# Attention layer 1 of a graph network on one Trainium2 core: the query and key product with its operands exchanged

## The reference

```python
def rgat_conv(x, W, q, k, b, src, dst, etype, heads, out_ch, n_nodes):
    xr = jnp.einsum('nd,rdf->rnf', x, W)          # 3 relations x 256 nodes x 768
    oi = xr[etype, dst]
    oj = xr[etype, src]
    qi = oi @ q                                    # 4 query numbers per row of xr
    kj = oj @ k                                    # 4 key numbers per row of xr
    alpha = jax.nn.leaky_relu(qi + kj, NEG_SLOPE)
    m = jax.ops.segment_max(alpha, dst, num_segments=n_nodes)
    e = jnp.exp(alpha - m[dst])
    z = jax.ops.segment_sum(e, dst, num_segments=n_nodes)
    a = e / (z[dst] + EPS)
    msg = (a[:, :, None] * oj.reshape(-1, heads, out_ch)).reshape(-1, heads * out_ch)
    out = jax.ops.segment_sum(msg, dst, num_segments=n_nodes)
    return out + b
...
h = rgat_conv(x, W1, q1, k1, b1, src, dst, edge_type, HEADS1, OUT1, n)
h = jax.nn.elu(h)
out = rgat_conv(h, W2, q2, k2, b2, src, dst, edge_type, HEADS2, OUT2, n)
```

## Time and profile before

| | |
|---|---|
| median of 3 runs | 1147.63 us (1140.77 to 1148.91) |
| the profiled execution's own time | 1147.76 us |
| its span in the profile | 1146.0 us |
| PE busy | 1086.9 us (95%) |
| VectorE busy | 766.9 us (67%) |
| ScalarE busy | 572.0 us (50%) |
| mean granted TensorE clock | 0.981 of full speed |

### The profile page before, as it was taken

How to read it: one execution, slowest core, us unless ns; L and a number is a source line. 1 busy time by engine, 2 the same in 40 slices (tenths; PEclk the granted TensorE clock), 3 DMA queues, 4 the chain that set the end, 5 groups by cost and what they waited for, 6 DMA issues and landing times.

```text
span 1146.0 us, 17627 instructions
## 1 busy us (share of the span) xinstructions
PE 1086.9 (95%) x7440; PEld 902.1 (79%) x7440; DVE 766.9 (67%) x1082; ACT 572.0 (50%) x602; POOL 180.1 (16%) x96
## 2 busy tenths in 40 slices
PE   7999998999899999998999989899999999999987
PEld 5889986444699964446679889858999999999984
DVE  7994763888643148885355374755888888888752
ACT  0433225888433258884234353424666666666640
POOL 2434602555100015552000000000000000000000
PEclk9999999999899999999999799999999999999998
DMA  8043285211044372210234103507777777777720
GB/s 292 11 132 119 84 270 154 60 56 56 1 166 166 120 220 57 74 56 1 83 132 179 49 1 131 196 1 259 255 234 250 244 249 246 247 246 240 246 98 28
DMA packets 82322, 163.47 MB, mean 143 GB/s; under 512 B 4034, under 2 KB 60126, under 8 KB 81950
## 3 DMA queue, kind: packets, MB, share of 16 engines
q1 hardware_dynamic: 80736, 151.86, 39.8%
q0 software_dynamic: 1504, 10.44, 3.5%
HBM read 158.64 MB, written 0.80 MB: 139 GB/s over the span
## 4 chain that ended last, share of the span: by engine, by line
PE 66%; DVE 20%; ACT 7%; issue 4%; DMA 1%; POOL 1%; SPq 0%; DVEq 0%; ACTq 0%; POOLq 0%
PE PS L977 12%; PE PS L835 7%; PE PS L717 6%; PE PS L469 6%; PE PS L631 4%; PE PS L733 4%; PE PS L456 4%; DVE Wlo L1783 3%; PE PS L607 3%; PE PS L991 3%; PE PS L960 3%; ACT Whi L1308 3%; PE PS L538 2%; DVE PRD L1554 2%; PE PS L896 2%
## 5 line engine op out<-in xcount | busy, mean ns | idle before, releaser
L1783 DVE TENSOR_TENSOR Wlo<-W,Whi 128x2304 fp32r<-128x2304 f32 x68 | 173.8, 2557 | 43.4 <-ACT Whi L1308 43.4
L1308 ACT CAST Whi<-W 128x2304 fp32r<-128x2304 f32 x68 | 144.4, 2125 | 0.1
L977 PE MATMUL PS<-Whi,Mhi 128*128 128x384 f32 x408 | 139.6, 342 | 3.5 <-DVE Mlo L1812 3.5
L977 PE MATMUL PS<-Wlo,Mhi 128*128 128x384 f32 x408 | 136.6, 335 | 0.0
L977 PE MATMUL PS<-Whi,Mlo 128*128 128x384 f32 x408 | 136.6, 335 | 0.0
L428 POOL TENSOR_TENSOR PRDP<-arena 128x1024 f32<-128x1024 f32 x48 | 114.6, 2388 | 122.8 <-PE PS L733 88.3
L717 PE MATMUL PS<-QH,SEL 128*128 128x512 f32 x384 | 116.8, 426 | 9.6 <-DVE arena L1554 3.6
L717 PEld LDWEIGHTS PS<-QH,SEL 128*128 128x128 f32 x384 | 65.4, 190 | 60.6 <-DVE PRD L1554 22.7
L1169 ACT ACTIVATE arena<-PS 128x1024 f32<-128x1024 f32 x96 | 98.5, 1026 | 27.7 <-PE PS L717 27.7
L1169 ACT ACTIVATE PS<-PS 128x1024 f32<-128x1024 f32 x96 | 98.0, 1020 | 0.0
L977 PEld LDWEIGHTS PS<-Whi,Mhi 128*128 128x128 f32 x408 | 76.7, 188 | 8.3 <-DVE Mlo L1812 8.3
(11 more groups left out here) (274 smaller groups left out, 2403.2 us busy)
## 6 DMA issues: line engine op xcount, KB each, us to landing
W<-in_L_rel SPq DMA_DIRECT2D x68, 1152.0 KB, 5.6
W<-in_W_rel SPq DMA_DIRECT2D x6, 2304.0 KB, 9.2
W<-in_W SPq DMA_DIRECT2D x6, 2304.0 KB, 8.5
arena<-in_qU SPq DMA_DIRECT2D x96, 128.0 KB, 2.6
W<-in_WqT SPq DMA_DIRECT2D x4, 2304.0 KB, 9.2
W<-in_W_root SPq DMA_DIRECT2D x2, 2304.0 KB, 13.4
W<-in_WgT SPq DMA_DIRECT2D x2, 2304.0 KB, 9.0
QH<-QH POOLq DMA_DIRECT2D x2, 1536.0 KB, 10.0
```

What stands on the lines that cost most here:

```text
L977: mm = pe.matmul(PS[:, 4 + s % 2, 0:HALF], MS[a][mb][:, k, j * P:(j + 1) * P], WS[b][w % 3][:, k, :], start=n == 0, stop=n == 17)
L1308: nc.scalar.copy(WS[0][w % 3][:], W[(FIRST34 + r) % 2][:, :, q * HALF:(q + 1) * HALF]).then_inc(w_hi, 1)
L1783: V.tensor_tensor(WS[1][w % 3][:], W[(FIRST34 + r) % 2][:, :, q * HALF:(q + 1) * HALF], WS[0][w % 3][:].bitcast(F32), ALU.subtract).then_i ...
```

## The change

`queries_keys(r)` makes the 128 x 8 block of `qk1` stationary and lets a 128 x 256 block of `XT` move, so that its result is eight rows of 256 nodes (partitions 0 to 7 of bank 3 for relations 0 and 1, of bank 4 for relation 2). VectorE negates these rows into a new tile `qkR` in two pieces. `spread_keys` of layer 1 selects one row of `qkR` with a broadcast column of the identity (8 x 128, stationary) while 8 x 256 blocks of `qkR` move. The queries are turned back by six transposes (`turn_queries`), issued between the spreads of head 0 and head 1, and VectorE copies them to `qkN`. `turn_rows(2)` is issued ahead of `queries_keys(1)` instead of behind it. Layer 2 keeps its code.

```diff
+        qkR = put("qkR", [2 * HEADS1, R3 * NODES], F32, 36)
...
-            pool.wait_ge(qk_done, 1)
+            pool.wait_ge(qk_done, R3)
...
-                for t in range(NT):
-                    at = (t * R3 + r) * 2 * HEADS1
-                    for k in range(KC):
-                        mm = pe.matmul(PS[:, 3, at:at + 2 * HEADS1], XT[:, r, k, t * P:(t + 1) * P], qk1[:, k, :],
-                                       start=k == 0, stop=k == KC - 1)
-                return mm
+                for k in range(KC):
+                    mm = pe.matmul(PS[0:2 * HEADS1, 3 + r // 2, (r % 2) * NODES:(r % 2 + 1) * NODES], qk1[:, k, :], XT[:, r, k, :],
+                                   start=k == 0, stop=k == KC - 1)
+                mm.then_inc(qk_done, 1)
+
+            def turn_queries():
+
+                for c in range(R3 * NT):
+                    r, t = divmod(c, NT)
+                    mm = pe.transpose(PS[:, 6, 2 * HEADS1 * (R3 * t + r):2 * HEADS1 * (R3 * t + r + 1)],
+                                      qkR[:, c * P:(c + 1) * P], ident[0:2 * HEADS1, 0:2 * HEADS1])
+                mm.then_inc(rows_turned, 1)
...
                     queries_keys(0)
+                    turn_rows(2)
                     queries_keys(1)
-                    turn_rows(2)
-                    queries_keys(2).then_inc(qk_done, 1)
+                    queries_keys(2)
...
-                    pe.wait_ge(qkn_copied, 1)
+                    pe.wait_ge(qkr_copied, 2)
...
-                    for c in range(R3 * NT):
+                    for r in range(R3 if l == 0 else 0):
+                        mm = pe.matmul(PS[:, 4 - h % 2 * 2 + r // 2, (r % 2) * NODES:(r % 2 + 1) * NODES],
+                                       ident[0:2 * HEADS1, HEADS1 + h:HEADS1 + h + 1].to_broadcast([2 * HEADS1, P]),
+                                       qkR[:, r * NODES:(r + 1) * NODES], start=True, stop=True)
+                    for c in range(R3 * NT if l == 1 else 0):
...
                 for h in range(min(H, 2)):
                     spread_keys(h)
+                    if l == h == 0:
+                        turn_queries()
...
-                    dve.wait_ge(qk_done, 1)
-                    V.tensor_scalar(qkN[:], PS[:, 3, 0:NT * R3 * 2 * H].rearrange("p (t r h) -> p t r h", t=NT, r=R3),
-                                    -1.0, None, ALU.mult).then_inc(qkn_copied, 1)
+                    dve.wait_ge(qk_done, 2)
+                    V.tensor_scalar(qkR[:, 0:2 * NODES], PS[0:2 * H, 3, :], -1.0, None, ALU.mult).then_inc(qkr_copied, 1)
+                    dve.wait_ge(qk_done, 3)
+                    V.tensor_scalar(qkR[:, 2 * NODES:], PS[0:2 * H, 4, 0:NODES], -1.0, None, ALU.mult).then_inc(qkr_copied, 1)
+                    dve.wait_ge(rows_turned, 1)
+                    V.tensor_copy(qkN[:], PS[:, 6, 0:NT * R3 * 2 * H].rearrange("p (t r h) -> p t r h", t=NT, r=R3)
+                                  ).then_inc(qkn_copied, 1)
```

More of the change, by code:

```diff
@@ L269, in build @@
         elu_min, elu_exp = sem("elu_min"), sem("elu_exp")
+        qkr_copied, rows_turned = sem("qkr_copied"), sem("rows_turned")
         qkb_in, row_half, qk_made = sem("qkb_in"), sem("row_half"), sem("qk_made")
```

## The result

The ratio to the kernel before is **0.9965, 95% interval 0.9949 to 0.998**: faster by 0.35%, some 4.0 us of 1147.6, and inside the 1% that was called no change. The interval stands for 2.3 to 5.9 us. The medians of 20 runs each are 1140.51 us (1135.72 to 1146.6) and, before, 1145.63 us (1137.89 to 1150.56), which is 5.1 us apart. The prediction said 1143.0, 1138 to 1151.

The account below looks back on a forecast made before the run. The serial stretch to ScalarE's first scores, 631 to 650 us, was taken as the bound. -6.0 there and +1.4 given back in the units made -4.6 from 1147.63: 1143.0 us, 8-in-10 range 1138 to 1151.

Parts of the forecast that it names:

- If the clock holds: Layer 1 products of queries and keys: PE stays at 2.4 GHz, new records 0.216 us apart; chance 0.55, 1143.0 us.
- Rival (a): New products: the clock falls there too, near 636, and the change is slower, 1149.2 to 1151.1 us; chance 0.28.
- Rival (b): New products: exchanged operands are no cheaper, each record paying an unhidden load, +5.0 us, 1146.6 us; chance 0.07.
- The stage: Serial stretch of products, negation, spread and copy: first scores start at 644.0 instead of 650.01, -6.0 us.
- the negation with its handovers: Between products and first spread: the second piece of VectorE's negation is new on the path, 0.5 us.
- turning back: Six query transposes behind the first spread: between 0.8 and 2.6 us, taken as 0.7 behind its last record.
- The give-back: First units behind the spreads: PE idles, the clock may fall, losing 0 to 3.5 us; 1.4 taken.
- the third and fourth spread cost the same number of moving columns: Later spreads in the units: 1.3 us against 1.34 before, so no change in time.
- the upper bound: Units: 3.5 us lost if the clock is low for one weighted sum, two turned units and a slow spread.
- the median is 1147.63, the same for this purpose: Whole kernel: the starting time, 1147.63 us, treated as equal to the profiled execution's 1147.76.
- The rule that transposes don't count for the clock: Moved transposes between relations 0 and 1: not counted as work keeping the clock up, so they help it fall; 1150 us.
- Equal clocks: Relation 0 products: 24 old records about 3.0 us at the high clock, new form 2.6 us, only slightly cheaper.

Follow-up runs that it names:

- no filling: Changed kernel without the 30 keep-busy matmuls behind the spreads; ratio 0.9996 to the kernel before.
- order alone: Kernel before with one edit: transposes of relation 2 issued ahead of the products of relation 1; run twice, ratios 0.9987 and 1.0003 to the kernel before.

## Why the prediction was right

- **The clock in the products.** "If the clock holds" was the forecast's condition, at 0.55, and it held, in every profile with the full moving side (eight kernels, nine profiles; the changed kernel has two) and even over 16 us. With the old products it fell in all three profiles without fillers. Rival (a) fell. Rival (b) fell as well: the new records start 0.216 us apart, exactly the value used. What it is in the exchange that kept the clock up stays open. It changes three things at once (256 moving columns for 8, 8 stationary columns for 128, half as many records), and no run tells them apart.
- **The stage.** Forecast -6.0, measured -6.2 in the profiled execution. Products and transposes 626.29 to 636.36 are 10.1 (9.9 forecast), the negation with its handovers 0.50 (0.5), spread 1.56 (1.5), turning back 0.34 on the chain (0.6 behind the spread), copy with handovers 0.26 (0.3). The transposes with 8 moving columns followed one another at 0.06 us, not at the 0.13 taken.
- **The give-back.** 1.4 was taken between 0 and 3.5, all of it for a low clock under the first units. The clock did fall, at 640, but the 30 keep-busy matmuls stood under it and the units lost nothing by it. The 0.35 us that they did lose (40.56 - 40.22) comes from a term that the prediction put at nothing, "the third and fourth spread cost the same number of moving columns": at the high clock the spread with 8 rows and the sum behind it took 1.49 + 2.16 us against 1.34 + 1.97. The "no filling" run shows that the upper bound was real.
- **Profile against median.** The last term, "the median is 1147.63, the same for this purpose", was off in two ways. The median of 20 runs is 1145.63, so that -4.6 from there would have been 1141.0. And one profile is not the average. The profiled execution of before had a mean clock of 0.981 where the mean of 92 was 0.9856, and that of the changed kernel 0.990 where its own was 0.9885. So 18.95 us is probably on the long side of what the old stage takes; no second profile of that kernel shows it, but the "order alone" pair has 14.4 and 18.5 from one program.
- **Luck.** The net gain by the start of layer 2 was 5.9 us in one pair of profiles, and the whole gain 4.0 by the ratio. The forecast of 4.6 came so near because a give-back that was 1.0 too large stood in for what one profile overstates and for the 2.5 us lost at the end. The mechanism was right, that closeness was luck.
- **The transposes.** The rule that transposes don't count for the clock, put forward for rival (a), did no harm: in every kernel with the new product and the new order they stood between the products, and the clock did not fall there. Whether they count at all was not told apart.
- **Equal clocks.** The prediction had the new form slightly cheaper at an equal clock, "about 3.0 us" for 24 old records. Its own row, 30 records in 3.0 us, gives 2.4. Measured at the high clock, 24 old records took 2.58 us (order alone) and the 12 new ones 2.69, so the new form is slightly dearer. This had no weight in the sum, which counts the new records by their own price.

## What to carry to other kernels

Where matmuls of a few moving columns follow one another for some microseconds, look at the granted clock in windows before counting instructions: exchanging the operands so that the long side moves can cost as much PE time at an equal clock and still pay. A serial stage passes its gain on (here 5.9 of 6.2 us), but a filling of keep-busy matmuls behind it is part of the bargain; here it was worth 3.0 us in the profile and about the whole gain in the time. Keep an eye on the small side, too: spreads with 8 stationary rows cost more than those with 128, and a low stretch came behind them. One profile is one draw of the clock: compare the mean granted clock of many executions before a stage gain is taken for a gain in time.

## What the runs showed of the hardware

- Through products with 128 x 8 stationary and 256 moving float32 columns the clock stayed at 2.4 GHz for 16 us (with 2 us of transposes among them). Two spreads with 8 x 128 stationary and the same moving side, 3 us together, were followed by a fall to 1.2 GHz in each of four profiles; with 128 x 128 at the same place it fell in none of four. The number of stationary rows is what differs there; few stationary columns went with no fall. I had not expected the two to differ.
- At 2.4 GHz a spread of six records with 8 stationary rows took 1.49 us on the chain and one with 128 rows 1.30, and the weighted sum behind it 2.16 against 1.96.
- The same program (the order alone) had its low stretch begin near 638.1 and last some 7 us in one execution, and begin near 635 and last until past 651 in another, for 4.1 us of difference in one stage.
- Six transposes of 8 x 128 with 8 moving columns add 0.34 us to the chain.
